# Attention and gated feed-forward block, one core: softmax weights transposed in 32x32 blocks on VectorE and put together by SBUF-to-SBUF transfers, instead of on TensorE

## What is computed

```python
q = (x @ Wq + bq).reshape(b, h, t, dh)
k = (x @ Wk + bk).reshape(b, t, h, dh).transpose(0, 2, 3, 1)
v = (x @ Wv + bv).reshape(b, t, h, dh).transpose(0, 2, 1, 3)
logits = jnp.einsum('bhtd,bhds->bhts', q, k) * scale
mask = jnp.triu(jnp.full((t, t), -jnp.inf, dtype=x.dtype), k=1)
weights = jax.nn.softmax(logits + mask, axis=-1)
out = jnp.einsum('bhts,bhsd->bhtd', weights, v).transpose(0, 2, 1, 3).reshape(b, t, h * dh)
attention = out @ Wo + bo
ffn = einsum('bsh,dh->bsd', silu(gate) * up, w_down)      # gate, up = xn @ w_gate.T, xn @ w_up.T
return x + attention + ffn
```

## Time and profile before

| | |
|---|---|
| median of 3 runs | 2152.1 us (2151.52 to 2152.87) |
| the profiled execution | 2149.1 us, of which the span of the profile is 2147.3 us |
| busy | TensorE 98%, its weight load 88%, DVE 64%, ACT 51%, POOL 49% |
| TensorE clock, mean granted | 0.996 of full |
| HBM | 80.9 MB read, 50.3 MB written |
| first phase | to about 500 us; the rest is the second phase |

### The profile page before, as it was taken

One profiled execution on the slowest core, in us unless ns is written; L12 is line 12 of the kernel. 1 busy time (PEld: TensorE's weight loads), 2 busy tenths in 40 slices (PEclk: granted clock), 3 DMA queues, 4 the chain that ended last, 5 costly groups with the idle time before them and its releaser, 6 DMA issues.

```text
span 2147.3 us, 36441 instructions
## 1 busy us (share of the span) xinstructions
PE 2104.9 (98%) x13169; PEld 1897.7 (88%) x13169; DVE 1381.5 (64%) x3040; ACT 1101.5 (51%) x2410; POOL 1061.8 (49%) x1192
## 2 busy tenths in 40 slices
PE   7999999999999999999999999999999999999998
PEld 6888888878999999999999999899999989999997
DVE  7211111116777777777777777777777777777776
ACT  4333223224555555555555555555555555555554
POOL 4223232235555555555555555555555555555543
PEclk9999999999999999999999999999999999999999
DMA  6333333343111111121111122111111221111100
GB/s 225 102 108 108 89 108 108 108 129 95 35 35 36 35 35 63 52 81 36 36 35 36 35 74 71 49 43 35 40 35 35 74 74 35 36 35 37 46 16 20
DMA packets 136449, 133.58 MB, mean 62 GB/s; under 512 B 5536, under 2 KB 122448, under 8 KB 134992
## 3 DMA queue, kind: packets, MB, share of 16 engines
q1 hardware_dynamic: 136272, 131.25, 19.3%
HBM read 80.90 MB, written 50.33 MB: 61 GB/s over the span
## 4 chain that ended last, share of the span: by engine, by line
PE 92%; DVE 3%; DMA 2%; issue 1%; POOL 1%; ACT 1%; SPq 0%; DVEq 0%; POOLq 0%; ACTq 0%
PE s_ps L905 36%; PE o_ps L1083 19%; PE m_ps L905 15%; PE t_ps L1065 12%; PE t_ps L905 8%; PE o_ps L905 2%; DMA q_dram<-raw_w 1%; DMA wk_raw<-in_L_attn_Wk 1%; DVE xn_sb L777 1%; DVE stats L750 0%; PE t_ps L933 0%; DMA out<-y 0%; DVE sil L821 0%; ACT raw_w L653 0%; DVE wq_lo L799 0%
## 5 line engine op out<-in xcount | busy, mean ns | idle before, releaser
L603 POOL TENSOR_SCALAR prob<-prob,inv_sum 128x128 f32<-128x128 f32 (+7 forms) x512 | 382.6, 747 | 699.0 <-DVE inv_sum L879 699.0
L870 DVE TENSOR_REDUCE neg_max<-s_ps 128x1 f32<-128x128 f32 (+7 forms) x512 | 388.0, 758 | 17.5
L710 ACT ACTIVATE prob<-s_ps,neg_max 128x128 f32<-128x128 f32 (+7 forms) x512 | 381.6, 745 | 25.2 <-DVE neg_max L870 25.2
L1065 PE MATMUL t_ps<-ident,prob 128*128 128x128 f32 x2304 | 345.7, 275 | 11.3 <-POOL prob L603 7.0
L732 ACT ACTIVATE pT_diag_hi<-t_ps 128x128 fp32r<-128x128 f32 (+3 forms) x512 | 222.7, 435 | 193.3 <-PE t_ps L1065 193.3
L1065 PEld LDWEIGHTS t_ps<-ident,prob 128*128 128x128 f32 x2304 | 267.5, 140 | 53.1 <-POOL prob L603 13.7
L905 PE MATMUL s_ps<-k_hi,q_hi 128*128 128x384 f32 (+5 forms) x768 | 301.8, 393 | 0.8 <-ACT prob L710 0.8
L895 DVE TENSOR_TENSOR pT_diag_lo<-t_ps,pT_diag_hi 128x128 fp32r<-128x128 f32 (+3 forms) x512 | 246.5, 481 | 58.0 <-ACT pT_diag_hi L732 57.9
L905 PE MATMUL s_ps<-k_hi,q_lo 128*128 128x384 f32 (+5 forms) x768 | 262.7, 342 | 0.0
L905 PE MATMUL s_ps<-k_lo,q_hi 128*128 128x384 f32 (+5 forms) x768 | 261.7, 341 | 0.0
L547 POOL TENSOR_TENSOR q_lo<-q_raw,q_hi 128x512 fp32r<-128x512 f32 x128 | 199.5, 1559 | 10.7
(11 more groups left out here) (163 smaller groups left out, 5454.1 us busy)
## 6 DMA issues: line engine op xcount, KB each, us to landing
q_dram<-raw_w SPq DMA_DIRECT2D x64, 512.0 KB, 3.2
q_raw<-q_dram SPq DMA_DIRECT2D x64, 512.0 KB, 3.5
wk_raw<-in_L_attn_Wk SPq DMA_DIRECT2D x64, 128.0 KB, 3.7
wv_raw<-in_L_attn_Wv SPq DMA_DIRECT2D x32, 256.0 KB, 3.9
wo_raw<-in_L_attn_Wo SPq DMA_DIRECT2D x32, 256.0 KB, 2.7
x_sb<-in_L_attn_x SPq DMA_DIRECT2D x8, 512.0 KB, 9.1
xnT_dram<-xnT_a_hi SPq DMA_DIRECT2D x8, 512.0 KB, 3.1
xnT_dram<-xnT_a_lo SPq DMA_DIRECT2D x8, 512.0 KB, 3.9
```

Source lines behind the costliest of these rows:

```text
L603: eng.tensor_scalar(prob[:, j % 3, 0:L], prob[:, j % 3, 0:L], inv_sum[:, j % 4:j % 4 + 1], 1.0, ALU.mult, ALU.mult).then_inc(s_norm, 1)
L710: eng.activation(prob[:, j % 3, 0:L], s_ps[j % 2][:, c0:c1], ACT.Exp, bias=neg_max[:, j % 4:j % 4 + 1], accum_out=row_sum[:, j % 4:j % 4 + ...
L870: eng.tensor_reduce(neg_max[:, g % 4:g % 4 + 1], s_ps[g % 2][:, c0:c1], AX_X, ALU.max, negate=True).then_inc(s_max, 1)
L1065: ins = eng.transpose(t_ps[tb % 2][:, slot * P:(slot + 1) * P], prob[:, g % 3, kt * P:(kt + 1) * P], ident[:, :])
```

## The change

The softmax weights are no longer transposed by TensorE. After POOL has scaled a row tile, DVE transposes each 32x32 block of it in place within its quarter of the partitions (`stage`), and when the four row tiles of a half (`kc`) are done, SP issues 16 transfers, one for each pair of source and destination quarter (32 partitions, 512 or 1024 elements each), which lay the blocks in their places in `pT_lo` (`exchange`). ACT then copies each tile in fp32r as `pT_hi`, and POOL (tiles 0 to 3, 6, 7) or DVE (tiles 4, 5) subtracts it in place. Since this takes longer, V is multiplied later (`PV_AT`: 11 for half 0, 15, 16, 17 for half 1), and the splits have steps of their own (`SPLIT_AT`). Mask and maximum are one instruction, which writes the negated masked row back to PSUM over all its columns. The query is split in the first phase on ACT and DVE, one head for each `gate_up` piece, and stored as two arrays of 512 KB per head (`qs_dram`), which the second phase loads; in the last chunk the query projection goes ahead of the gate. Pieces of K, V and y take three PSUM banks in turn instead of sharing with the scores.

```diff
-PV_AT = {7: (0, 0, 1), 8: (0, 1, 4), 11: (1, 0, 2), 12: (1, 2, 4), 13: (1, 4, 8)}
+PV_AT = ((11, 0, 0, 4), (15, 1, 0, 2), (16, 1, 2, 4), (17, 1, 4, 8))
+O_AT = (12, 18)
+SPLIT_AT = ({9: (0, 1), 10: (2, 3)}, {13: (6, 4), 14: (7, 5)})
+ON_DVE = (4, 5)
+K_AT = (0, 1)
+V_AT = (-6, -2, 2, 3)
+Y_AT = (5, 6, 12, 13)
...
+        SPLITS_IN = {c: c - 1 for c in range(1, NC - 1)}
+        SPLITS_IN[NC - 1] = NC - 1
...
+            def store_qs(n):                                        # SP
+                eng.wait_ge(s_qlo, n + 1)
+                for part in range(2):
+                    eng.dma_start(qs_dram[part, n], qs_stage[part][:, n % 2].bitcast(F32)).then_inc(s_qsst[n % 2], 16)
+
+            def split_heads(c, alongside):
+                load_q_raw(QH * c)
+                load_q_raw(QH * c + 1)
+                for h in range(QH):
+                    alongside(h)
+                    store_qs(QH * c + h)
+                    if h + 2 < QH:
+                        load_q_raw(QH * c + h + 2)
...
+            def exchange(n, kc):
+                eng.wait_ge(s_t, NI * n + VT * (kc + 1))
+                if n:
+                    eng.wait_ge(s_pv, pv_chunk(n - 1, kc))
+                for src in range(NB):
+                    for dst in range(NB):
+                        eng.dma_start(pT_lo[kc][32 * dst:32 * (dst + 1), src].bitcast(F32),
+                                      stage[kc][32 * src:32 * (src + 1), dst]).then_inc(s_land[kc], 16)
...
+            def q_hi(n):                                            # ACT, first phase
+                eng.wait_ge(s_qrload[n % 2], 16 * (n // 2 + 1))
+                if n >= 2:
+                    eng.wait_ge(s_qsst[n % 2], 32 * (n // 2))
+                eng.activation(qs_view(0, n), q_raw_view(n), ACT.Copy).then_inc(s_qhi, 1)
...
-                    for bank in range(i // VT + 1):                 # ACT, second phase
-                        tb = t_banks_through(j - 1) + bank
-                        eng.wait_ge(s_t, tb + 1)
-                        eng.activation(pT_written(pT[0], i, bank), t_ps_used(tb, i, bank), ACT.Copy)\
-                           .then_inc(s_thi, 1)
+                for n, kc, i in tiles_split(g):
+                    if i == split_order[kc][0]:
+                        eng.wait_ge(s_land[kc], 16 * TRANSFERS * (n + 1))
+                    eng.activation(hi_tile(kc, i), raw_tile(pT_lo, kc, i).bitcast(F32), ACT.Copy)\
+                       .then_inc(s_phi[kc], 1)
...
-                    eng.tensor_tensor(diagonal, diagonal, mask[:, :], ALU.add).then_inc(s_masked, 1)
-                    eng.wait_ge(s_masked, g + 1)
-                    eng.tensor_reduce(neg_max[:, g % 4:g % 4 + 1], s_ps[g % 2][:, c0:c1], AX_X, ALU.max,
-                                      negate=True).then_inc(s_max, 1)
+                    eng.tensor_tensor_reduce(out=row, in0=row, in1=mask[:, T - L:T], scale=-1.0, scalar=BIG,
+                                             op0=ALU.add, op1=ALU.min, accum_out=neg_max[:, g % 4:g % 4 + 1])\
+                       .then_inc(s_max, 1)
...
+                    eng.transpose(stage[kc][:, :, i - VT * kc, 0:i + 1, :].rearrange("p b k t -> p k b t"),
+                                  prob[:, j % 3, 0:(i + 1) * P].rearrange("p (k b t) -> p k b t", b=NB, t=32))\
+                       .then_inc(s_t, 1)
...
+                if c == NC - 1:                                     # TensorE, first phase
+                    project_q(c)
```

426 lines of the change are left out of this document (211 added, 215 removed).

## The result

The changed kernel takes **2853.6 us** (median of four runs, 2851.3 to 2856.5), the kernel before 2151.8: a ratio of 1.326, 95% interval 1.324 to 1.329. The forecast was 2300, with a range up to 2400. The direction was right and the size far off. The profiled execution has a span of 2849.4 us.

A forecast was written before the change was run, and what follows sets the result against it. The weights' road of half 1, through the exchange, was taken as the bound at 26.0 us a head; 511 + 100 (query) + 20 (rest) + 4.8 + 64 x 26.0 = 2300 us, range 2055 to 2400.

The forecast's parts named there:

- TensorE bounds before, and its relief comes only if the weights' road is no longer than a head: Second phase: TensorE at 98% bounds; removing transposes saves at most 3.96 us a head, 253 us in all.
- Loads of the other engines: Second phase, per head: DVE 19.3 us and POOL below 18, against TensorE's 21.6; none becomes the bound.
- rival B: Second phase: DVE becomes the bound through slow fused instructions or block transposes; 2268 us and more, up to 2500; chance 0.10.
- X = 12.0 us: Exchange of half 1, from DVE's transpose of tile 7 to landing: 12.0 us, data taken at 200 GB/s.
- it hides: Exchange of half 0: half the bytes and as long a window, so it adds no time.
- SP's other loads wait behind the exchange, which costs nothing: SP's queue, second phase: loads behind the exchange cost nothing, since Wk is wanted only for the next head.
- Landing to PV 7.1 us: From half 1's landing to TensorE's product with V: copies, subtractions and scaling on ACT, DVE and POOL take 7.1 us.
- TensorE 5.0 us: TensorE's part of half 1's loop: key tiles, scores and a K piece take 5.0 us a head.
- the clock after a wait: TensorE in half 1's loop: a clock of 0.50 after waiting adds up to 2.5 us a head, kept for the range.
- Rival A: Exchange at or near full rate: period 22.1 to 23.3 us, typically 2070 us; threshold 270 GB/s; chance 0.32.
- Some reordering slack: Half 1's loop: reordering lowers the period from 26.4 to 26.0 us a head.
- First phase +100 us: Query split in the first phase: loads and stores priced at 364 GB/s add 100 us, from 60 to 150.

The follow-up runs named there:

- run 3: The changed kernel with SP's loads of Wk, Wv and Wo ahead of the exchange of half 1, and all low parts on DVE: 2567.4 us.
- run 2: The changed kernel with all low parts of the transposed weights on DVE, none on POOL: 2758.8 us.
- run 1: The changed kernel with SP issuing the loads of Wk, Wv and Wo ahead of the exchange of half 1: 2680.4 us.
- run 5: The changed kernel with exchange transfers over 128 partitions, blocks left out of place: 2839.5 us with 16 for a half, 2667.3 us with four.
- run 6: The kernel of run 3 with ACT issuing 8 of the 16 transfers of half 1 and SP the others: 2975.3 us.
- run 7: The kernel of run 3 with four transfers of 128 partitions for a half, blocks left out of place: 2558.8 us.
- run 9: The kernel before with only the query split in the first phase, stored and loaded as high and low part: 2343.9 us.

## Why the prediction was wrong, step by step

- **TensorE bounds before, and its relief comes only if the weights' road is no longer than a head**: right. The transposes left, and no engine is above 74%.
- **Loads of the other engines**: the fused instruction and the block transpose came as forecast; rival B fell. POOL's tile 7 took 2364 ns (forecast 2.4). DVE's tiles 4 and 5 were mis-sized, 1852 ns on average for 0.86: the price was taken from a row in which POOL did nothing of the kind beside it, and run 3 brings it back to 816 and 946 ns. This step failed too: 95 us alone (run 2), 113 on top of run 1.
- **X = 12.0 us**: 12.2 in the head shown and 13.0 on average, but what ends it is not the rate. SP's issue takes 0.59 us for such a transfer and 0.04 between two, where the earlier trace rows has 0.38 for a load; 16 make 10.05 us, and landing 2.1 more. Wide transfers changed nothing in X (run 5), and half 0, with half the bytes, took as long (16 issues, 10.5 us). So the forecast "it hides" was too cheap as well: SP issues for 20 us of each head. The assumed rate was not far off all the same: with the issue shared, the DMA engines are full at 226 GB/s (run 6), where 200 was taken. Two limits lie within a microsecond of each other, and the number came out right by luck: the prediction had the one that did not end last. By the Trainium skill (page "SBUF — State Buffer", section "Door 1: The DMA port swizzle") the number of ports reached bounds such a transfer, with 189 GB/s measured for 1 MiB on 32 partitions. Run 6 agrees in kind, with 226 GB/s, and so does run 5, where 128 partitions carried 201 GB/s at a share of 0.59.
- **"SP's other loads wait behind the exchange, which costs nothing"**: this step failed. It asked only when Wk is wanted, not what POOL has queued behind the split of Wk. It cost 2.7 us a head, 173 us (run 1).
- **Landing to PV 7.1 us**: 11.4 measured (11.6 on average), 7.3 (7.6) in run 3, with the two faults above out. The overlap of DVE and POOL and the wait for Wk were missing. That 7.3 is near 7.1 does not confirm the terms: in run 3 POOL subtracts nothing, and its 2.4 us for tile 7, which the prediction adds, are replaced by DVE's subtractions.
- **TensorE 5.0 us**: 7.9 in the head shown, 7.2 on average (6.5 in run 3). The prediction named the clock after a wait, priced it at 2.5 us a head from the earlier trace rows, and kept it for the range although its own loop left TensorE idle in each head. It belonged in the sum: 2.2 us a head here, 1.5 in run 3.
- **Rival A and its threshold**: its rate is not to be had with 32 partitions: the DMA engines were full at 226 GB/s in run 6, and its threshold was 270. And run 7 shows that even with X = 7.5 us the period would have been 29, not 22. Three things stood in the way at once (the wait for Wk, DVE beside POOL, the low clock), and behind them a second loop, the lag of one step between DVE's low parts and PV, which the prediction did not look for. "Some reordering slack" had no row behind it.
- **First phase +100 us**: +195 (run 9). It was priced by bytes at 364 GB/s, 4.3 us a head. In the trace a pair takes 10.4 us, 5.2 a head, over a load of 5.2, two passes of 2.0 (1.1 and 1.2 at unit step) and two stores in two slots, and the projection waits for its own stores behind those of the split. Eight heads beside `gate_up` took 43.8 us (247.5 to 291.3) where 34.5 were forecast, with the DMA engines at 0.87 and 312 GB/s; the chunk is 81 us where it was 57.
- **The sum**: the mean period in run 3 is 28.9 us, 2.9 above the forecast 26.0. So 2300 + 95 (query) + 64 x 2.9 = 2581, against 2567 measured; the two edits explain the other 286. Of the 2.9 us TensorE's part is 1.5, X 1.1, landing to PV 0.5 and the "reordering slack" 0.4, less 0.6 for hand-overs (which the measured parts contain) and DVE. The clock is about half of it; that the head shown above has 2.9 us in TensorE alone is a coincidence.

## What to carry to other kernels

Price a transfer by its issue as well as by its bytes: sixteen small ones on one queue cost 10 us here, with 64 KB each as with 128, and everything in that queue, and everything queued behind a wait on it elsewhere, moves by as much. Then ask what the DMA engines can carry at that width: a second issuer shortened X by about one us only, since they were full. When a loop has been found, ask what the next one is before believing a saving: cutting the exchange by 4.8 us a head gave 9 us in one order of steps and 161 in another. And take durations of two-input subtractions on DVE only from rows with the same neighbour on POOL.
